# Output stage: weight rounding without VectorE, last chunk tile by tile, tables fetched early, half of up's first tiles scaled by GpSimd

## The reference

```python
x = x + tanh(g_xattn) * attention(layernorm(x), ctx, mask, Wq, bq, ..., Wo, bo)
x = x + tanh(g_ffn) * ffn(layernorm(x), W1, b1, W2, b2)

def sym_quantize(w):                          # W1 is 2048 x 512, W2 is 512 x 2048
    scale = maximum(max(abs(w)) / 127.0, 1e-8)
    return clip(round(w / scale), -127, 127), scale

def affine_quantize(x):                       # one scale and zero point for the whole tensor
    scale = maximum((max(x) - min(x)) / 255.0, 1e-8)
    zp = clip(round(-min(x) / scale) - 128, -128, 127)
    return clip(round(x / scale) + zp, -128, 127), scale, zp

def qlinear(x, W, b):
    return ((xq - zp) @ wq.T) * (sx * sw) + b

h = gelu(qlinear(layernorm(x), W1, b1))       # exact gelu
out = qlinear(h, W2, b2)
```

## Time and profile before

| what | us |
|---|---|
| median of 3 runs | 1582.28 |
| the runs | 1577.43 to 1584.48 |
| the profiled execution | 1579.47 |
| its span, first to last instruction | 1577.7 |

### The profile page before, as it was taken

The page is one execution under the profiler, slowest core; times in us unless marked ns, Lnnn a source line. Parts: engine busy times, 40 slices in busy tenths (PEclk is TensorE's granted clock), DMA queues, the critical chain, the costliest instruction groups (busy, mean ns, idle before and its releaser), DMA issues. The chain is left out here.

```text
span 1577.7 us, 34377 instructions
## 1 busy us (share of the span) xinstructions
PE 1402.0 (89%) x14575; PEld 579.6 (37%) x14598; DVE 1291.7 (82%) x1337; ACT 868.2 (55%) x932; POOL 930.1 (59%) x693
## 2 busy tenths in 40 slices
PE   3899999659999999999999999999969839893997
PEld 1344444313333333333333333333324314441443
DVE  7777776388888888888888888888529969999786
ACT  3233323216666666667766767666732458763453
POOL 7222111028888888888888888888936669900000
PEclk9899999889999999999999999999989959996999
DMA  9466555570332133312332133300038506653986
GB/s 293 114 225 214 181 179 192 135 203 9 85 81 66 35 85 88 79 38 65 86 82 62 39 85 82 85 22 13 21 120 277 202 27 255 249 217 113 335 291 220
DMA packets 126921, 207.06 MB, mean 131 GB/s; under 512 B 11956, under 2 KB 65204, under 8 KB 125248
## 3 DMA queue, kind: packets, MB, share of 16 engines
q1 hardware_dynamic: 119616, 187.73, 38.6%
q0 software_dynamic: 3424, 8.95, 1.8%
q10 hardware_dynamic: 3744, 8.39, 1.5%
HBM read 124.29 MB, written 72.35 MB: 125 GB/s over the span
## 5 line engine op out<-in xcount | busy, mean ns | idle before, releaser
L718 POOL TENSOR_TENSOR x<-x 128x512 f32<-128x512 f32 x512 | 673.6, 1328 | 141.3 <-ACT x L759 134.9
L786 DVE TENSOR_REDUCE row_max<-ring 128x1 f32<-128x1024 f32 x512 | 609.9, 1214 | 99.5 <-PE ring L620 97.5
L759 ACT ACTIVATE x<-ring 128x1024 f32<-128x1024 f32 x512 | 514.1, 1024 | 240.5 <-PE ring L682 239.5
L644 PE MATMUL o_acc<-x,v 128*32 128x512 f32 x2048 | 264.4, 592 | 3.2 <-ACT x L759 2.3
L682 PE MATMUL ring<-ffn_w_int 128*32 128x512 f16 x2560 | 194.2, 380 | 6.0 <-DVE row_max L786 6.0
L620 PE MATMUL ring<-ffn_w_int 128*32 128x512 f16 x2560 | 193.8, 379 | 6.1 <-DVE row_max L786 6.1
L620 PE MATMUL ring<-x 128*32 128x512 f16 x1536 | 119.2, 392 | 26.9 <-DMA v<-scratch_V 15.5
L653 PE MATMUL sum_acc<-x,ones 128*32 128x512 f32 x1024 | 132.1, 592 | 1.5 <-POOL x L718 1.5
L1146 PE MATMUL hid<-xqT,ffn_w_int 128*128 128x512 bf16 x499 | 119.6, 394 | 10.2 <-ACT xqT L1176 8.0
L1355 PE MATMUL down<-ffn_w_int,hq 128*128 128x512 bf16 x502 | 113.4, 383 | 15.2 <-ACT hq L1341 14.5
L682 PE MATMUL ring<-x 128*32 128x512 f16 x1536 | 115.4, 380 | 4.2 <-DVE row_max L786 4.1
(11 more groups left out here) (181 smaller groups left out, 2063.9 us busy)
## 6 DMA issues: line engine op xcount, KB each, us to landing
scratch_G<-gelu SPq DMA_DIRECT2D x56, 512.0 KB, 2.6
g_in<-scratch_G SPq DMA_DIRECT2D x28, 1024.0 KB, 5.9
x<-in_ctxT SPq DMA_DIRECT2D x8, 1024.0 KB, 6.9
x<-in_x SPq DMA_DIRECT2D x8, 1024.0 KB, 8.8
scratch_V<-x SPq DMA_DIRECT2D x32, 256.0 KB, 3.1
v<-scratch_V SPq DMA_DIRECT2D x16, 512.0 KB, 8.5
out<-x POOLq DMA_DIRECT2D x7, 1024.0 KB, 7.3
ffn_w_int<-scratch_QH SPq DMA_DIRECT2D x20, 256.0 KB, 4.1
```

The source lines that it names most:

```text
L644: last = nc.tensor.matmul(oacc[h * DK:(h + 1) * DK], v[buf][:, kt, h * DK:(h + 1) * DK], prob[:, s % 2, h, part], tile_position=(0, h * DK ...
L718: nc.gpsimd.tensor_tensor(pair[:, s % 2, h], prob[:, s % 2, h, 0], prob[:, s % 2, h, 1], ALU.add).then_inc(pair_done, 1)
L759: nc.scalar.activation(prob[:, s % 2, h], ring[slot][:], ACT.Exp, scale=SM_SCALE).then_inc(exp_done, 1)
L786: nc.vector.tensor_reduce(mraw[:, i:i + 1], ring[slot][:], AX.XY, ALU.max).then_inc(max_done, 1)
```

## The change

In `stage_output`:

- ScalarE multiplies a weight piece by the inverse scale and adds MAGIC in the same instruction, which rounds. GpSimd then clips the rounded value between MAGIC - 127 and MAGIC + 127 (`clip_w`, now in GpSimd's list, where `round_off` was). VectorE's `clip_w` and the semaphore `w_scaled` are gone. GpSimd's loop over quarters is written out.
- For the last chunk VectorE takes the tiles one after the other: residual, statistics, maximum and minimum of one tile, then the next tile. The other chunks keep their order, without the clip.
- ScalarE runs a square root on one column (`spare`) before the first weight piece, and a Gelu on one column after the standard deviation, at the end of the block.

In `stage_up`, GpSimd scales tiles 1, 3, 5 and 7, ahead of tile 8 (`odd_scaled`). ScalarE scales tiles 0, 2, 4 and 6.

```diff
@@ -881,13 +881,14 @@
         std = sb("ln2_std", [P, TILES], F32)
+        spare = sb("table_spare", [P, 1], F32)
         banks = [ctx.enter_context(nc.psum_tensor(f"out_proj{i}", [P, D], F32)) for i in range(8)]
...
         w_max_ready, w_all_ready, w_step = sem("w_max_ready"), sem("w_max_all_ready"), sem("w_scale_step")
-        w_inv_ready, w_scaled, w_clipped, w_rounded, w_done = sem("w_inverse_ready"), sem("w_scaled"), sem("w_clipped"), sem("w_rounded"), sem("w_integers_ready")
+        w_inv_ready, w_clipped, w_rounded, w_done = sem("w_inverse_ready"), sem("w_clipped"), sem("w_rounded"), sem("w_integers_ready")
         end_step = sem("ln2_step")
@@ -915,19 +916,19 @@
-            def round_off(b, s):
-                pool.wait_ge(w_clipped, 2 * b + s + 1)
-                nc.gpsimd.tensor_tensor(w[:, s], w[:, s], k.magic[:].to_broadcast([P, F]), ALU.add).then_inc(w_rounded, 1)
+            def clip_w(b, s):
+                pool.wait_ge(w_rounded, 2 * b + s + 1)
+                nc.gpsimd.tensor_scalar(w[:, s], w[:, s], MAGIC + 127.0, MAGIC - 127.0, ALU.min, ALU.max).then_inc(w_clipped, 1)
             pool.sem_inc(xb_ready, 2)
-            with pool.Fori(0, B - 1) as b:
+            for b in range(B - 1):
                 for s in range(2):
-                    round_off(b, s)
+                    clip_w(b, s)
                     pool.wait_ge(x_loaded[s], 16 * (b + 1))
...
             for s in range(2):
-                round_off(B - 1, s)
+                clip_w(B - 1, s)
@@ -955,9 +956,9 @@
                     act.wait_ge(w_loaded[s], 16 * (b + 1))
-                    nc.scalar.activation(w[:, s], w[:, s], ACT.Copy, scale=w_inv[:, s:s + 1]).then_inc(w_scaled, 1)
+                    nc.scalar.activation(w[:, s], w[:, s], ACT.Identity, scale=w_inv[:, s:s + 1], bias=k.magic[:, 0:1]).then_inc(w_rounded, 1)
                 for s in range(2):
-                    act.wait_ge(w_rounded, 2 * b + s + 1)
+                    act.wait_ge(w_clipped, 2 * b + s + 1)
                     nc.scalar.activation(out[:, s, bass.ds(b, 1)].rearrange("p b n -> p (b n)"), w[:, s], ACT.Identity,
@@ -967,12 +968,14 @@
                 load(0, s)
+            nc.scalar.activation(spare[:], k.eps[:], ACT.Sqrt)
             act.wait_ge(w_inv_ready, 1)
...
             nc.scalar.activation(std[:], mv[:, :, 1], ACT.Sqrt, bias=k.eps[:, 0:1]).then_inc(std_ready, 1)
+            nc.scalar.activation(spare[:], k.eps[:], ACT.Gelu)
@@ -983,10 +986,6 @@
-            def clip_w(n):
-                dve.wait_ge(w_scaled, n + 1)
-                nc.vector.tensor_scalar(w[:, n % 2], w[:, n % 2], -127.0, 127.0, ALU.max, ALU.min).then_inc(w_clipped, 1)
@@ -995,19 +994,33 @@
                     rows = ext[:].rearrange("p m (b n) -> p m b n", b=B)
-                    for t in range(4):
+                    def residual(t):
                         dve.wait_ge(projected, 4 * (n + 2) + t + 1)
...
                                                        in1=k.xb[s][:, t], op0=ALU.mult, op1=ALU.add).then_inc(x2_ready, 1)
-                    clip_w(n)
-                    for t in range(4):
+                    def statistics(t):
                         dve.wait_ge(x2_ready, 4 * (n + 2) + t + 1)
...
                         nc.vector.bn_stats(stats[:, t], x2[:, t]).then_inc(stats_done, 1)
-                    for m, op in enumerate((ALU.max, ALU.min)):
-                        nc.vector.tensor_reduce(rows[:, m, bass.ds(b, 1), 4 * s:4 * (s + 1)].rearrange("p b t -> p (b t)"), x2, AX.X, op,
-                                                negate=(m == 1)).then_inc(x2_topped, 1)
+                    def extrema(t, many):
+                        for m, op in enumerate((ALU.max, ALU.min)):
+                            nc.vector.tensor_reduce(rows[:, m, bass.ds(b, 1), 4 * s + t:4 * s + t + many].rearrange("p b t -> p (b t)"),
+                                                    x2[:, t:t + many], AX.X, op, negate=(m == 1)).then_inc(x2_topped, 1)
+                    if n < 2 * B - 1:
+                        for t in range(4):
+                            residual(t)
+                        for t in range(4):
+                            statistics(t)
+                        extrema(0, 4)
+                    else:
+                        for t in range(4):
+                            residual(t)
+                            statistics(t)
+                            extrema(t, 1)
                     dve.wait_ge(stats_done, 4 * (n + 1))
@@ -1016,7 +1029,7 @@
             nc.vector.scalar_tensor_tensor(out=k.shift2[:], in0=mv[:, :, 0], scalar=-1.0, in1=k.rstd2[:], op0=ALU.mult, op1=ALU.mult).then_inc(end_step, 1)
-            dve.wait_ge(x2_topped, 4 * B)
+            dve.wait_ge(x2_topped, 2 * (2 * B - 1) + 8)
             for m in range(2):
@@ -1042,6 +1055,7 @@
         ring = [ctx.enter_context(nc.psum_tensor(f"hid{i}", [P, 2, HALF], F32)) for i in range(RING)]
+        odd_scaled = sem("first_odd_tiles_scaled")
         first_scaled, first_rounded, first_quantized = sem("first_tiles_scaled"), sem("first_tiles_rounded"), sem("first_tiles_quantized")
@@ -1085,6 +1099,8 @@
             pool.wait_ge(coef_ready, 2)
+            for i in range(1, PER, 2):
+                nc.gpsimd.tensor_scalar(xs[:, i], k.x2[:, i], coef[:, 0, i:i + 1], coef[:, 1, i:i + 1], ALU.mult, ALU.add).then_inc(odd_scaled, 1)
             for i in range(PER, TILES):
@@ -1092,7 +1108,8 @@
                 if i == PER + 3:
-                    pool.wait_ge(first_scaled, PER)
+                    pool.wait_ge(first_scaled, PER // 2)
+                    pool.wait_ge(odd_scaled, PER // 2)
                     bias(0)
@@ -1108,7 +1125,7 @@
             for i in range(PER):
-                dve.wait_ge(first_scaled, i + 1)
+                dve.wait_ge(odd_scaled if i % 2 else first_scaled, i // 2 + 1)
                 nc.vector.tensor_scalar(xs[:, i], xs[:, i], par.hi, MAGIC, ALU.min, ALU.add).then_inc(first_rounded, 1)
@@ -1161,7 +1178,7 @@
             act.wait_ge(coef_ready, 2)
-            for tiles in range(4):
+            for tiles in (0, 2):
                 scale(tiles)
@@ -1169,7 +1186,7 @@
                         scale(tiles)
-                        tiles += 1
+                        tiles += 2
                     act.wait_ge(xq_turned, i + 1)
```

## The result

| | before | after |
|---|---|---|
| median, us | 1582.28 | 1575.03 |
| the runs, us (7 of each) | 1577.43 to 1584.48 | 1571.51 to 1577.91 |
| the profiled execution, us | 1579.47 | 1571.72 |
| its span, us | 1577.7 | 1569.9 |

The ratio of the times is 0.9953, with a 95% interval from 0.9935 to 0.997. The change makes the kernel 7.25 us faster, a little under 0.5%. The forecast was 1576.2.

What follows compares the result with a forecast made beforehand. VectorE was taken to finish the output stage behind TensorE, which would pace without the clip. Terms -7.2 + 0.5 + 0.6 = -6.1 us gave 1573.4 for the profiled execution, 1576.2 as median, range 1572 to 1581.

Steps and rivals of the forecast that it cites:

- The clip leaves VectorE: Output stage: without the weight clip VectorE comes down to TensorE's pace and the last aggregation starts earlier, -7.2 us.
- Last chunk tile by tile: Output stage, last chunk: VectorE has a backlog, so the new order is worth nothing, 0.2 us lost.
- The weight chain: Output stage: ScalarE's merged pass and GpSimd's clip of 3.1 us stay covered; cost 0, bounds 0 and +0.5 us.
- Early tables: Output stage: early square root gains 0; the Gelu after the deviation delays the stage's end, +0.5 us (bounds 0 and +0.5).
- The scales on GpSimd: Start of `stage_up`: GpSimd's scales take turns with VectorE and lengthen its 16 instructions, +0.6 us (0 to +3.1).
- rival 2: Start of `stage_up`: each early GpSimd scale blocks VectorE whole, +3.1 there; sum -3.6 us, 1578.7; chance 0.11.
- Rival (1): Nothing gives back: stage's end doesn't wait for ScalarE, turns in `stage_up` cost nothing; gain 7.2 us, 1575.1; chance 0.18.
- (4): Output stage: something unseen, such as late x, holds VectorE at each chunk, so no gain; 1582 us; chance 0.05.
- rival (3): Output stage: GpSimd becomes the pacer, slower from 7.1 us per clip; at 8 us per clip, 1588; chance 0.04.

Runs made afterwards that it cites:

- e4: Kernel before with the new weight chain alone (no tile order, early tables or scales on GpSimd): 1574.23 us, ratio 0.9937 to the kernel before.
- e5: Changed kernel without a third of TensorE's products in the output stage (8 per tile instead of 12): 1562.90 us, one run.
- e3: Changed kernel with the last chunk in the order of the others: 1575.40 us, one run.
- e10: Changed kernel with 24 products per tile instead of 12, last chunk tile by tile: 2.58 us from last residual to last aggregation.
- e11: Changed kernel with 24 products per tile instead of 12, last chunk in the others' order: 7.42 us from last residual to last aggregation.
- e2: Changed kernel without the one-column Gelu after the standard deviation: 1575.85 us, one run.
- e9: Changed kernel without the end-of-block Gelu, ScalarE scaling all eight first tiles, GpSimd's later tiles held until VectorE finishes those eight: 1570.53 us.
- e1: Changed kernel with ScalarE scaling all eight first tiles of `stage_up` again: 1575.44 us, one run.
- e8: Changed kernel without the end-of-block Gelu, GpSimd's later tiles held until VectorE finishes the first eight, GpSimd's four scales kept: 1570.47 us.

## Why the prediction was right, and where it was not

In the terms of the profiled execution the sum was -6.1 us, and it moved by 7.75. Step by step:

**The clip leaves VectorE: right, in mechanism and size.** Forecast -7.2. The last aggregation moved by 7.47, of which 0.21 was there at the start: -7.26. Chunk 6's fourth residual was to start at 1245.29 and chunk 6 to end at 1253.01; the trace has 1245.08 and 1252.80, each 0.21 earlier, as the start is. e4 shows that this part alone makes the gain, e5 that TensorE holds the pace.

**Last chunk tile by tile: right.** Forecast 0.2 lost. A tile takes 2.56 (2.57 foreseen), the whole order costs 0.16 (e3). A slip that changed nothing: at 10.36 us a chunk the third tile comes at 1245.29 + 3 x 2.59 = 1253.06, so at 1253.01 two tiles were waiting and not three; each still came before its turn. That it would pay without a backlog is shown by e10 and e11.

**The weight chain: right that it costs nothing, the size of the clip wrong.** It takes 1.9 us instead of 3.1; the rows of 128x512 that I scaled up were a poor guide to it. The bounds of 3.1 to 4.2 did not hold it. This did no harm, as the weights were finished 9.35 us before the deviation. ScalarE's first pass, now with scale and bias, was counted at no change; it takes 2.09 where it took 2.00. TensorE shows no gap from later loads.

**Early tables: right.** Square root 0 (e4), Gelu at the end of the block +0.36 against a forecast of +0.5 (e2). The term came out smaller because the spare activation on one column takes 0.20, where I had put 0.32, the row of 32 columns. The wait from ScalarE's end to the next stage was 0.30, as foreseen. The Trainium skill, ScalarE: Activation LUTs, section "What ACT_TABLE_LOAD costs", gives about 1.28 us for the load and another 1.38 for a drain. Here the load takes 1.28, begins 0.02 after the deviation ends and is followed by the activation 0.01 after it; no such drain shows on this path. By the page's sum the stage would have ended some 1.4 us later, an estimate that the trace does not bear out.

**The scales on GpSimd: this step failed, in sign.** I put them at +0.6 (0 to +3.1); they gain 0.87, outside the bounds. I had let one VectorE instruction pass per scale, 0.86 for it. In the trace two pass, 0.72 and 0.47, and from start to start they take 1.15 together (1271.24, 1271.88). I had also counted the first free pairs that get dearer, and some return from later long turns, but far too little of it, since I let only half as many instructions pass before those turns begin: GpSimd begins its later tiles at 1273.97, after 4.06 us of scales, and so the first of its additions, beside which a VectorE instruction takes 1.26 instead of 0.47, comes at 1276.36. The first long turn is the eleventh of the 16 (1276.48); in the kernel before it was the seventh (1281.18). With the trace's durations the term would have been three long pairs against two, 0.95 less, and 0.1 more for the first pairs. The lower bound of 0 assumed that a turn costs VectorE the same whatever GpSimd runs.

The Trainium skill, SBUF — State Buffer, section "SBUF: two separate sides", says that the pair of ports is held for a whole instruction and the loser blocks. The trace agrees that the two engines wait for each other (1.26 us where VectorE alone takes 0.48), and e9 shows the whole price, 4.64 us. But read plainly, the rule made this edit a loss of up to 3.1 us (rival 2), and the edit gained 0.87. By the rows above, what decided the sign is how many instructions of one engine pass between two of the other.

**The sum.** With the terms as measured: -7.26 + 0.36 - 0.87 = -7.8. Rival (1), nothing gives back, had the better number (-7.2, or 1575.1), but not for its reason: the Gelu does give back, and the scales gain. Rivals (2) and (4) are excluded by e1 and e4, rival (3) needs a clip 3.4 times as long.

**What passed on unforeseen.** The forecast took a shift ahead of the first extremum to reach the end whole. It does, but by luck, as two shifts cancel: 1.05 us more are gained between the first Gelu and the first extremum of `stage_up`, and 1.17 are given back in the first chunk of `stage_down`. Both go with the granted clock (last section); what sets the moment at which it rises stays open.

## What to carry to other kernels

When two engines are both busy all through a stage, taking work off the one that finishes last is worth only the way down to the other's pace; price it as the follower's new finish (here 7.26 us, from a clip whose eight instructions add up to 13.0), and then ask what the follower does after the last product. A finer order helps where the follower waits, at every chunk and not only the last: in the last chunk alone it lost 0.16 us, in all chunks it gained 3.5. Before offloading a small operation to GpSimd, look at which of its instructions VectorE meets and count from the rows how many pass per turn; here keeping GpSimd's later work out of VectorE's critical phase shortened that phase by 4.64 us, and handing it more of the work by 0.87.

## What the runs showed of the hardware

**Turns between VectorE and GpSimd depend on the instruction.** Alone, VectorE's 128x512 instruction takes 0.48 us. Beside GpSimd's scales a pair takes 1.15 instead of 0.92; a pair that meets GpSimd's addition (1276.36) takes 2.09. GpSimd pays too: the first of its four scales, ahead of VectorE, takes 0.77, and those beside VectorE up to 1.16.

**A GpSimd clip between two constants is cheap.** On 128x2048 it takes 1.9 us, where the addition of MAGIC to the same tile took 3.60.

**TensorE's clock rises a different time after its work begins.** Windows of 1 us of the kernel before, in the first products of `stage_up` and of `stage_down`, columns as in the earlier trace rows:

```profile
1296.00:1297.00 1.00, 1.00 (x4) 0.45 (x3) 0.00 (x0) 0.16 (x1) 1.00 (x2) 0.50 0.00 0
1297.00:1298.00 1.00, 1.00 (x9) 0.52 (x8) 0.00 (x0) 0.16 (x1) 1.00 (x1) 0.93 0.97 397
...
1453.00:1454.00 1.00, 1.00 (x4) 0.33 (x3) 1.00 (x2) 1.00 (x1) 0.00 (x0) 0.50 1.03 381
1454.00:1455.00 1.00, 1.00 (x5) 0.39 (x4) 1.00 (x2) 0.55 (x2) 0.00 (x0) 0.93 0.49 176
```

In `stage_down` the products began at 1450.77 before the change and at 1441.77 after it. The granted clock went from 0.50 (1.2 GHz) to 1.00 (2.4 GHz) just after 1454 and near 1447.5, and TensorE was busy without a break until then. So it worked at the lower clock for some 3.4 us before and 5.7 after. It does half as much there, so half of the difference, 1.2 us, is what this can account for: the 1.17 that were given back. The other traces agree. In e8, with 2.7 us at the lower clock, the first residual comes 15.33 us after the first product; in e9, with 6.0 us, 16.99. All 14 traces lie on this line, at 0.50 us for each us at the lower clock, to within 0.02.

The first products of `stage_up`, before and after:

```profile
1291.73 6.08 PE L1146 MATMUL hid<-xqT,ffn_w_int 128*128 128x512 bf16 x15 [1.15 <-ACT xqT L1176]
1283.39 5.41 PE L1163 MATMUL hid<-xqT,ffn_w_int 128*128 128x512 bf16 x16 [0.77 <-ACT xqT L1193]
```

The trace before has 15 products where the one after has 16, and the first Gelu follows VectorE's 16 instructions by 5.11 us in both. So the record of the first product seems to be missing before, and it began near 1291.35 (1289.85 + 1283.39 - 1281.89). The clock rose just after 1297 and just after 1287. That makes 5.8 us at the lower clock before and 3.7 after, and half of the difference is the 1.05 that were gained. This is worked out from rows; no run tried what makes the clock rise when it does.
